# One Mamba-plus-LoRA layer on one core: the second residual is carried by an identity in the weights, the turned tiles are copied by ScalarE, and the work is ordered by new shift tables

## The chip, the cores and the metric

The kernel runs on one core of one Trainium2 chip. The metric is device time in microseconds (us) of one execution. One execution was also taken with the hardware profiler; that one gives the rows shown here. Engines are named as in the profile: PE is TensorE (PEld its weight loads), DVE is VectorE, ACT is ScalarE, POOL is GpSimd, SP is SyncE, whose queue starts every DMA of this kernel.

## What is computed

Four sequences of 512 tokens with 1024 features, all in fp32. Each sequence passes a state-space mixer and then a small feed-forward product; a layer norm with residual follows each of the two.

```python
def mixer(x):                                  # D = 2048 channels, N = 16 states, R = 64
    u, gate = split(x @ W_in.T)
    u = silu(causal_conv4(u) + conv_b)
    dt, B, C = split(u @ Wx.T, [R, R + N])     # each root-mean-square normed
    delta = softplus(dt @ Wdt.T + dt_bias)
    state_t = exp(delta * A) * state_(t-1) + (delta * u) * B   # per channel and state
    y = sum_n state * C + u * D_param
    return (y * silu(gate)) @ W_out.T

x1 = layernorm(x + mixer(x))
out = layernorm(x1 + x1 @ W.T + b + lora(x1))  # lora: rank 8, 16, 32 or 64, chosen per token
```

The second residual, the `x1 +` in the last line, is what the change touches.

## The kernel before

**The scan.** The recurrence is cut into 256 units: sequence b (4), group g of 512 channels (4), state n (16), in that order. For one unit POOL multiplies `delta_u` by a broadcast row of B (stage `drive`, L1816, 128x2048), ACT makes four decays with exp (`decay`, L1604), DVE runs four scans (`scan`, L1347, 128x512), PE turns the result in four tiles (`turn`, L1166, four 128x128 matmuls for a tile), and each turned tile is multiplied by its C column and added to `y_acc`. That last step has two ways: DVE does it in one instruction (`add`, L1372), or ACT scales the tile into a buffer (`scale`, L1624) and POOL adds it (`sum`, L1821). The first unit of a group writes `y_acc` instead (`first`, ACT).

**The work beside it.** Beside the scans run the products of the other stages: `u_mm` and `g_mm` (the input product, from weights split in a rounded part and a rest: three matmuls for each of 8 k-tiles, L1198 to L1200, called a triple here), `o_mm` (the output product, L1221), `f_mm` (the feed-forward product, triples again), the layer norms, and everything that copies and turns their results. Weights are loaded by SP to `w_raw`, rounded by ACT (`w_high`, L1645), their rest is made by POOL (`w_low`, L1840), the pair is stored once (`w_store`) and loaded ready made later (`w_load`).

**The second residual before.** For sequences 0 to 2 the feed-forward product comes out with features on the partitions. ACT copies it from its bank with the bias (`f_copy`, L1717), PE turns it (`f_turn`), and DVE adds the turned tile to `rows`, which holds x1 (`f_add`, L1426, in one line with `o_add`, the same for the first residual). The last sequence is done in the tail with tokens on the partitions: POOL adds the bias to `rows` (`fr_bias`, L1850, 128x1024 four times), and DVE adds the product's bank to `rows` (`fr_add`, L1458).

**The order.** A planner (`Plan.arrange`) fixes the order of instructions on each engine when the program is built. Each piece has a due time, an assumed length, needs, and the buffers that it takes. An engine's next piece is the one with the earliest due time among those that are ready. Due times are shifted by two tables, `STAGE_SHIFTS` (by stage and sequence) and `JOB_SHIFTS` (by job), in half microseconds. Whether an add goes to DVE or to ACT and POOL is settled in the planner too, by which of the two comes up first:

```python
put("DVE", i + 5 - ADD_FIRST, 0.645, "add", (s, tt), [*turned, summed(s - 1, tt)])
put("ACT", i + 5 - ADD_FIRST, 0.575, "scale", (s, tt), turned, take=[("scaled", (s, tt))], ahead_of="POOL")
```

At run time each engine works through its list and waits on semaphores, so an engine never goes past a piece that is not ready. Three banks of PSUM serve all products and turns beside the scan. SP too takes its list in order: `wf_load` is one piece of the planner and four DMAs (32 for a half of the ready-made feed-forward weights), and waits for the last `o_mm` of sequence 2 (first half), or for the last turns of the scan (second half).

Of the kernel before, what the change touches and what calls it, by code (L numbers as in the profile page):

```python
# [11 lines left out]
P = 128  # L12
# [5 lines left out]
GT = 4  # L18
# [89 lines left out]
class Once:  # L108
# [5 lines left out]
    def wait_ge(self, semaphore, value):  # L114
# [6 lines left out]
    "x_load": (-143, 5, 23, 103, 59, -146, -93, 156),  # L121
    "x_high": (-158, -53, -68, -77),
    "x_first": (-47,),
    "raw_load": (-53, -72, -27, -113),
    "w_high": (-41,),
    "dt_rest": (77,),
    "w_store": (61,),
    "consts": (125,),
    "lora_high": (-124,),
    "lora_rest": (78,),  # L130
    "rows_load": (215, 5, -73, -29),
    "w_low": (-31,),
# [18 lines left out]
    "delta_mm": (-4, 0, 43, -100),
    "softplus": (-160, 108, 88, 101),
    "g_mm": (41, 5, 30, 51),
    "g_copy": (-140, 113, -79, -79),
    "g_silu": (-113, -50, -82, -77),
    "g_store": (121, 13, -155, 144),
    "x_low": (0, -66, -150, -51),
    "w_load": (0, 13, 3, 19, 102),
    "o_mm": (1, 9, 68, 97),
    "o_copy": (160, -157, -110, -4),  # L160
    "o_turn": (-155, -36, -39, 113),
    "o_add": (-94, -34, -64, -118),
    "ln1_stats": (-128, -147, 87),
    "ln1_sqrt": (49, 66, 8),
    "ln1_rstd": (-40, 50, 72),
    "ln1_bias": (-160, 14, 141),
    "ln1_norm": (-142, -53, 122),
    "x1_turn": (-97, -91, 10),
    "x1_high": (72, -272, -44),
    "x1_low": (-38, -323, -43),  # L170
    "route_mm": (-60, -51, -112, -144),
    "route_lift": (-27, 90, 130, 122),
    "route_rows": (-218, -122, -45, -71),
    "route_max": (-235, -15, -97, 54),
    "route_exp": (-215, -5, 113, 63),
    "route_pick": (-213, -48, -93, -108),
    "route_mask": (29, -26, -160, 148),
    "route_turn": (-119, -109, -156, -135),
    "lora_cols": (24, 51, 34, 201),
    "lora_low": (-86, -2, -54, -65),  # L180
    "f_mm": (-3, 44, 177),
    "f_lora": (39, -152, 66),
    "f_copy": (-47, -77, -104),
    "f_turn": (9, -134, -75),
    "f_add": (17, -56, 34),
    "ln2_stats": (35, -86, -37),
    "ln2_sqrt": (72, 66, -50),
    "ln2_rstd": (-68, -132, 42),
    "ln2_bias": (-213, -233, 147),
    "ln2_norm": (-78, 157, -153),  # L190
    "y_high": (0, 0, 0, 0, 0, 0, 0, 0, 81, 7, 123, 147, 73, 28, 56, -100),
    "y_rest": (0, 0, 0, 0, 0, 0, 0, 0, 68, 83, 9, 120),
    "y_low": (0, 0, 0, 0, 0, 0, 0, 0, 0, 0, 0, 0, -97, 84, 88, 108),
    "or_mm": (115, 120, -35, 32),
    "or_table": (0, 0, 0, -95),
    "or_add": (5, 68, -150, 99),
    "or_stats": (91, 269, 66, 139),
    "or_sqrt": (-57, 119, -57, 111),
    "or_rstd": (106, 34, 36, 26),
    "or_norm": (-90, 194, 118, -14),  # L200
    "or_vnorm": (144, -40, -96, -233),
    "xr_turn": (-121, -93, 157, -95),
    "xr_high": (-43, -137, 105, -259),
    "xr_low": (-147, 191, 53, -56),
    "fr_table": (0, 0, 0, -136),
    "wf_load": (155, 59),
    "bias_load": (-76,),
    "fr_bias": (-75, 43, -76, 106),
    "fr_mm": (-208, -16, 70, 93),
    "fr_lora": (127, 69, -34, -125),  # L210
    "fr_add": (170, 150, -79, 97),
    "fr_stats": (-63, 17, 81, 129),
    "fr_sqrt": (17, -135, -158, 72),
    "fr_rstd": (-144, -132, 65, -272),
    "fr_norm": (25, -57, 77, 66),
    "fr_vnorm": (-259, 28, -48, -132),
    "rows_store": (-181, -155, 86, -65),
    "fetch": (-93, 15, 53, -141),
    "du_head": (107,),
    "g_load": (123, -18, 140, 116),  # L220
    "y_turn": (-135, 27, -103, -23),
    "y_skip": (-99, -155, 72, -11),
    "y_gate": (-118, -158, 119, 135),
    "drive_begun": (45,),
    "drive_head": (-13,),
    "decay": (-38, -16, 69, -25),
    "scan": (62, -5, -1, 79),
    "turn": (9, -157, -104, -97),
    "first": (72, -16, 0, -111),
    "drive": (95, 12, 143, 2),  # L230
    "add": (-68, -10, -43, 61),
    "scale": (-170, 30, -148, -125),
    "sum": (-113, -1, 119, -228),
    "du": (-51, -70, -59, 22),
# [3 lines left out]
    "x": (-151, -131, 34, 142, -119, -114, 42, 149, 55, -3, 38, 57, 75, -2, 86, 93, -93, 27, 26, 3, 90, 96, 90, 99, -55, -71, -158, -128, 24, -36, 38, 135),  # L238
    "split": (
# [8 lines left out]
    ),  # L248
    "u": (-121, -90, 35, 105, -39, -35, 44, 86, 36, 140, 48, -158, -137, -113, 58, -30, -33, -44, -66, -132, 4, 33, 83, 77, -110, -142, 55, -29, 113, 139, -140, 104, 44, -19, -144, -113, -61, -155, -6, -4, 140, -85, -14, -10, -34, 60, 101, -20, 67, 65, -141, 22, -15, 127, -51, 152, 64, 128, 20, -134, 48, 112, 66, 105),
# [1666 lines left out]
```

## Time and profile before

| | |
|---|---|
| runs | 2136.52, 2137.46, 2137.69 us (median 2137.46) |
| profiled execution | 2135.3 us, its span 2133.5 us |
| first scan starts, last scan ends | 137.17 us, 2027.4 us |
| DVE busy between these two | 1859.08 of 1890.25 us |
| instructions | 30661 |

The span is what the profiler saw from the first to the last instruction; 1.8 us of the execution's time lie around it. The program has three stretches: a head, in which the first sequence's products are made and no scan can run; the long middle with the scans; and a tail, the last sequence's output product, layer norms and feed-forward product. A busy share is the union of an engine's instructions, so instructions that overlap in the pipeline of their engine count once there; the mean length of one instruction is somewhat more than the step from its start to the start of the next.

### The profile page before, as it was taken

The numbers are of one execution on the slowest core, as the hardware profiler recorded it, in microseconds if no ns is written. First come the engines' busy times: TensorE is split into PE (matmuls) and PEld (weight loads), VectorE is DVE, ScalarE is ACT, GpSimd is POOL, SyncE is SP. The second block draws the span as 40 slices with busy tenths as digits, with TensorE's granted clock in tenths as the row PEclk, the third lists the DMA queues.
The fourth block names the chain that finished last, engine by engine and source line by source line (L and its number), as shares of the span: only waits on it lengthen the run. The fifth ranks groups of instructions, "written<-read, shape, count | busy, mean of one in ns | idle before, by whom it ended". The sixth has DMA issues, their size and how long they took to land.

```text
span 2133.5 us, 30661 instructions
## 1 busy us (share of the span) xinstructions
PE 2024.4 (95%) x10528; PEld 1529.3 (72%) x10528; DVE 1965.2 (92%) x2379; ACT 1477.0 (69%) x2191; POOL 1811.0 (85%) x773
## 2 busy tenths in 40 slices
PE   7999999999989799999999997999999999899998
PEld 6877778877565477788775556878875557686686
DVE  3469999999999999999999999999999999999944
ACT  4488777787576777786876557677796666857622
POOL 4369988988999999888899998988799998789941
PEclk9999999999999999999999998999999999999999
DMA  8887856654333358765563333585464337455340
GB/s 283 275 296 263 268 193 192 207 176 129 96 102 111 106 170 257 244 196 170 170 190 113 106 104 104 169 285 169 147 202 114 108 97 248 138 166 154 109 144 40
DMA packets 168763, 363.22 MB, mean 170 GB/s; under 512 B 18656, under 2 KB 45408, under 8 KB 168608
## 3 DMA queue, kind: packets, MB, share of 16 engines
q1 hardware_dynamic: 168608, 361.26, 52.9%
q8 instruction: 84, 1.38, 0.3%
q14 instruction: 71, 0.58, 0.1%
HBM read 292.35 MB, written 68.85 MB: 169 GB/s over the span
## 4 chain that ended last, share of the span: by engine, by line
PE 27%; DVE 17%; issue 5%; ACT 2%; POOL 1%; DMA 1%; SPq 1%; DVEq 0%; POOLq 0%; ACTq 0%
DVE drive L1347 10%; PE bank L1221 8%; PE state_t L1166 7%; DVE y_acc L1372 4%; PE bank L1198 2%; PE bank L1200 2%; PE bank L1199 2%; DVE channels L1379 1%; PE bank L1166 1%; POOL drive L1816 1%; DVE ln_stats L1435 1%; DVE channels L1416 1%; DMA w_split<-w_split 1%; PE bank L1264 0%; SPq L1132 0%
## 5 line engine op out<-in xcount | busy, mean ns | idle before, releaser
L1816 POOL TENSOR_TENSOR drive<-delta_u,b_bcast 128x2048 f32<-128x2048 f32 x255 | 1168.8, 4585 | 82.6 <-PE state_t L1166 76.3
L1347 DVE TENSOR_TENSOR_SCAN drive<-decay,drive 128x512 f32<-128x512 f32 x1024 | 1192.5, 1207 | 4.5 <-ACT decay L1604 3.9
L1604 ACT ACTIVATE decay<-delta,a_sb 128x512 f32<-128x512 f32 x1024 | 692.7, 688 | 352.8 <-DVE drive L1347 347.8
L1166 PEld LDWEIGHTS state_t<-identity,drive 128*128 128x128 f32 x4096 | 479.9, 142 | 251.0 <-DVE drive L1347 72.7
L1166 PE MATMUL state_t<-identity,drive 128*128 128x128 f32 x4096 | 574.9, 277 | 57.8 <-DVE drive L1347 32.7
L1198 PE MATMUL bank<-cols_high,w_split 128*128 128x512 f32 (+1 forms) x1240 | 527.2, 425 | 28.4 <-POOL w_split L1840 16.5
L1372 DVE SCALAR_TENSOR_TENSOR y_acc<-state_t,c_rows,y_acc 128x512 f32<-128x512 f32 x702 | 498.0, 736 | 20.7 <-PE state_t L1166 19.4
L1200 PE MATMUL bank<-cols_high,w_split 128*128 128x512 f32 (+1 forms) x1240 | 491.0, 396 | 0.0
L1199 PE MATMUL bank<-cols_low,w_split 128*128 128x512 f32 (+1 forms) x1240 | 488.5, 394 | 0.0
L1221 PE MATMUL bank<-channels,w_raw 128*128 128x512 f32 x896 | 421.5, 593 | 2.5 <-ACT delta L1709 2.0
L1821 POOL TENSOR_TENSOR y_acc<-y_acc,scaled 128x512 f32<-128x512 f32 x258 | 332.5, 1289 | 73.1 <-ACT scaled L1624 70.3
L1198 PEld LDWEIGHTS bank<-cols_high,w_split 128*128 128x128 f32 (+1 forms) x1240 | 235.2, 190 | 73.8 <-issue 19.5
L1200 PEld LDWEIGHTS bank<-cols_high,w_split 128*128 128x128 f32 (+1 forms) x1240 | 234.1, 189 | 54.4 <-issue 0.6
L1199 PEld LDWEIGHTS bank<-cols_low,w_split 128*128 128x128 f32 (+1 forms) x1240 | 236.3, 191 | 36.8 <-issue 0.7
L1221 PEld LDWEIGHTS bank<-channels,w_raw 128*128 128x128 f32 x896 | 153.2, 190 | 112.7 <-issue 109.9
L1624 ACT ACTIVATE scaled<-state_t,c_rows 128x512 f32<-128x512 f32 x258 | 175.8, 681 | 81.4 <-PE state_t L1166 46.9
L1840 POOL TENSOR_TENSOR w_split<-w_raw,w_split 128x512 fp32r<-128x512 f32 (+1 forms) x98 | 128.3, 1319 | 95.5 <-ACT w_split L1645 95.3
L1379 DVE SCALAR_TENSOR_TENSOR channels<-bank,conv_w_sb,channels 128x511 f32<-128x511 f32 (+2 forms) x192 | 142.7, 745 | 52.2 <-ACT channels L1653 47.6
L1604 ACT ACT_TABLE_LOAD x78 | 100.1, 1283 | 1.9 <-DVE drive L1347 0.6
L1645 ACT ACTIVATE w_split<-w_raw 128x512 fp32r<-128x512 f32 (+1 forms) x98 | 60.2, 619 | 39.2 <-PE decay L1285 10.4
L1836 POOL TENSOR_TENSOR channels<-channels,scratch 128x512 f32<-128x512 f32 x64 | 82.1, 1301 | 5.6 <-DVE channels L1416 4.4
L1829 POOL TENSOR_TENSOR delta_u<-delta,channels 128x512 f32<-128x512 f32 x60 | 75.7, 1288 | 1.8 <-ACT delta L1709 1.3
(226 smaller groups left out, 1441.4 us busy)
## 6 DMA issues: line engine op xcount, KB each, us to landing
w_split<-w_split SPq DMA_DIRECT2D x304, 512.0 KB, 4.3
b_bcast<-b_rows SPq DMA_DIRECT2D x256, 256.0 KB, 3.5
w_raw<-in_w_out SPq DMA_DIRECT2D x112, 256.0 KB, 3.0
w_raw<-in_w_in SPq DMA_DIRECT2D x64, 256.0 KB, 4.2
gates<-scratch SPq DMA_DIRECT2D x64, 256.0 KB, 3.8
scratch<-gates SPq DMA_DIRECT2D x64, 256.0 KB, 4.7
rows<-in_x_rows SPq DMA_DIRECT2D x4, 2048.0 KB, 10.7
out<-rows SPq DMA_DIRECT2D x16, 512.0 KB, 4.5
```

Of the source, the lines that this page charges most:

```text
L1166: last = engine.transpose(bank[0:tile.shape[1], i * P:(i + 1) * P], tile, identity[:, :])
L1198: engine.matmul(bank[:, :], high[:, k % WK, :], cols_high[:, k, :], start=first, stop=False)
L1199: engine.matmul(bank[:, :], high[:, k % WK, :], cols_low[:, k, :], start=False, stop=False)
L1200: engine.matmul(bank[:, :], low[:, k % WK, :], cols_high[:, k, :], start=False, stop=last).then_inc(signal[stage])
L1221: engine.matmul(bank[:, :], tile[:, k % WK, :], chan[s % 2][:, k, :], start=(k == tiles[0]), stop=(k == tiles[-1])).then_inc(signal["o_mm"])
L1347: engine.tensor_tensor_scan(state, decay[(GT * s + t) % DECAYS][:, :], state, 0.0, ALU.mult, ALU.add).then_inc(signal["scan"])
L1372: engine.scalar_tensor_tensor(y_acc[:, tt, :], bank[:, :], c, y_acc[:, tt, :], ALU.mult, ALU.add).then_inc(signal["add"])
L1379: m = engine.scalar_tensor_tensor(conv[:, back:T], bank[:, 0:T - back], conv_w[:, j, KC - 1 - back:KC - back], conv[:, back:T], ALU.mult, ...
L1604: engine.activation(decay[i % DECAYS][:, :], delta[:, g % 2, t, :], ACT.Exp, scale=a_sb[:, j, n:n + 1]).then_inc(signal["decay"])
L1624: engine.activation(scaled[:, :], bank[:, :], ACT.Copy, scale=c_rows[b % 2][:, tt, n:n + 1]).then_inc(signal["scale"])
L1816: engine.tensor_tensor(drive[key % DRIVES][:, :, :], du[:, :, :], row, ALU.mult).then_inc(signal["drive"])
L1821: engine.tensor_tensor(y_acc[:, tt, :], y_acc[:, tt, :], scaled[:, :], ALU.add).then_inc(signal["sum"])
```

## The change

The feed-forward weights get an identity added to them before they are split: for output tile h and k-tile h, POOL adds `identity` to a 128x128 part of `w_raw` (`w_eye`, eight in all, in the first use only; the stored weights carry it from then on). So the product already holds x1. `f_add` becomes a plain copy of the turned tile to `rows`, on ACT, with the same waits as before. In the tail `fr_bias` falls away: `fr_add` adds the bank to the bias tile instead of to `rows`, and takes over the waits that `fr_bias` had. Both shift tables are new in every entry, so the whole order is another one.

```diff
+def with_rows(what):
+    return F_TILE <= what[0] < ROUTE_TILE and (what[0] - F_TILE) // WK == what[1]
...
 STAGE_SHIFTS = {
-    "x_load": (-143, 5, 23, 103, 59, -146, -93, 156),
+    "x_load": (-45, -95, 18, 21, 133, 108, 80, 51),
...
-        put("ACT", due - 4, 0.13 + 0.4 * part, "w_high", w, [("raw_load", ("w", w))], take=[(pool, w)])
+        if with_rows(what):
+            put("POOL", due - 5, 0.4, "w_eye", w, [("raw_load", ("w", w))])
+        put("ACT", due - 4, 0.13 + 0.4 * part, "w_high", w, [("w_eye", w) if with_rows(what) else ("raw_load", ("w", w))], take=[(pool, w)])
...
-        put("DVE", due + 1.5, 0.585, name + "_add", key, [(name + "_turn", key), ("rows_load", key[0])] + (
+        put("DVE" if name == "o" else "ACT", due + 1.5, 0.585, name + "_add", key, [(name + "_turn", key), ("rows_load", key[0])] + (
...
-            put("POOL", at + 3, 2.4, "fr_bias", tt, [("bias_load", 0), *[("xr_turn", (tt, q)) for q in range(HT // GT)]])
...
-                put("DVE", due, 0.69, "fr_add", (tt, half), [("fr_lora", (tt, half)), ("fr_bias", tt)], give=[("bank", ("fr_mm", (tt, half)))])
+                put("DVE", due, 0.69, "fr_add", (tt, half), [("fr_lora", (tt, half)), ("bias_load", 0), *[("xr_turn", (tt, q)) for q in range(HT // GT)]], give=[("bank", ("fr_mm", (tt, half)))])
...
-                    engine.tensor_tensor(dst, bank[:, :], dst, ALU.add).then_inc(signal[stage])
+                    beside = dst if stage == "or_add" else ffn_bias[:, half * T:(half + 1) * T]
+                    engine.tensor_tensor(dst, bank[:, :], beside, ALU.add).then_inc(signal[stage])
...
+                elif stage == "f_add":
+                    s, h = key
+                    e.wait_ge(*done("f_turn", key))
+                    for h2 in range(HT):
+                        e.wait_ge(*done("x1_turn", (s, h2)))
+                    bank = banks[place["bank", ("f_turn", key)]]
+                    engine.activation(rows[:, :, h * P:(h + 1) * P], bank[:, :].rearrange("p (a q) -> p a q", a=TT), ACT.Copy).then_inc(signal["f_add"])
...
+                elif stage == "w_eye":
+                    at = (key[0][0] - F_TILE) % WK * P
+                    diagonal = raw[place["raw", key]][:, at:at + P]
+                    e.wait_ge(*done("raw_load", ("w", key)))
+                    engine.tensor_tensor(diagonal, diagonal, identity[:, :], ALU.add).then_inc(signal["w_eye"])
```

What the two orders hold that differs in number (everything else is there as often as before):

| engine, instruction | before | after |
|---|---|---|
| DVE `add` (y_acc from state_t) | 702 | 715 |
| DVE `o_add` and `f_add` (rows from a turned bank) | 64 | 40 |
| ACT `f_add` (copy to rows) | 0 | 24 |
| ACT `scale`, POOL `sum` | 258 each | 245 each |
| ACT table loads | 170 | 168 |
| POOL `fr_bias` | 4 | 0 |
| POOL `w_eye` | 0 | 8 |

Three places of the order are shown. The first is SP's queue from the program's start. `drive<-in_x_cols` loads one of the first sequence's eight k-tiles of x, `w_raw<-in_w_in` half of a weight tile; between them stand the constants, which are left out here but for the first and the last of twelve. Before:

```order
L1051 DMA drive<-in_x_cols 128x512
L1075 DMA w_raw<-in_w_in 128x512 x2
L1051 DMA drive<-in_x_cols 128x512
L1075 DMA w_raw<-in_w_in 128x512 x2
L1051 DMA drive<-in_x_cols 128x512 x5
L1045 DMA conv_w_sb<-in_conv_w 128x64
...
L1045 DMA drive<-in_lora_b 128x1024
L1051 DMA drive<-in_x_cols 128x512
```

and of the change:

```order
L1081 DMA w_raw<-in_w_in 128x512 x4
L1057 DMA drive<-in_x_cols 128x512 x7
L1051 DMA conv_w_sb<-in_conv_w 128x64
...
L1051 DMA drive<-in_lora_b 128x1024
L1057 DMA drive<-in_x_cols 128x512
```

The k-tile that is left for the end, behind the constants, was k = 7 before and is k = 4 now. Before, PE begins with two output tiles in turn, by k: ten triples stand ahead of the first that needs k = 7. Now it takes k = 0 to 3 of one tile and of a second, eight triples, and then needs k = 4.

The second place is ACT where the first scans are made ready: `delta<-bank` is softplus for two channel tiles, `decay<-delta` the exp of a scan, `dt_slot<-w_raw` and `w_split<-w_raw` round weights, `scratch<-bank` and `scratch<-scratch` copy a gate tile and take its silu. Before:

```order
L1693 ACTIVATE dt_cols<-bank,dt_ln_w_sb 128x512
L1666 ACTIVATE scratch<-bank 128x512
L1709 ACTIVATE delta<-bank,dt_bias_sb 128x512 x2
L1645 ACTIVATE w_split<-w_raw 128x512
L1604 ACT_TABLE_LOAD
L1604 ACTIVATE decay<-delta,a_sb 128x512 x2
L1645 ACTIVATE dt_slot<-w_raw 128x256
L1645 ACTIVATE w_split<-w_raw 128x512 x2
L1709 ACT_TABLE_LOAD
L1709 ACTIVATE delta<-bank,dt_bias_sb 128x512 x2
L1666 ACTIVATE scratch<-bank 128x512
L1604 ACT_TABLE_LOAD
```

and of the change:

```order
L1679 ACTIVATE scratch<-bank 128x512
L1706 ACTIVATE dt_cols<-bank,dt_ln_w_sb 128x512
L1658 ACTIVATE w_split<-w_raw 128x512
L1722 ACTIVATE delta<-bank,dt_bias_sb 128x512 x2
L1610 ACT_TABLE_LOAD
L1610 ACTIVATE decay<-delta,a_sb 128x512
L1658 ACTIVATE dt_slot<-w_raw 128x256
L1679 ACTIVATE scratch<-bank 128x512
L1658 ACTIVATE w_split<-w_raw 128x512
L1686 ACT_TABLE_LOAD
L1686 ACTIVATE scratch<-scratch 128x512 x2
L1722 ACT_TABLE_LOAD
```

The gate's silu with its table now stands ahead of the second softplus. On PE eleven gate triples stand ahead of the first `delta_mm` where eight stood (from the first `delta_mm` to the first turn of unit 1 both orders have the same 28 triples); on DVE only the first scan stands ahead of the second half of `delta_u` and `drive`, where two scans stood; on POOL 41 `w_low` stand ahead of the first `drive`, where 39 stood.

The third place is SP's queue in sequence 3, where the first half of the feed-forward weights is loaded (`w_f_early`, each row one fourth of a piece `wf_load`); `w_split<-w_split` is a `w_load`, `b_bcast` the row of B for a unit's `drive`. Before:

```order
L1078 DMA w_raw<-in_w_out 128x512
L1132 DMA w_f_early<-w_split 128x2x128 x16
L1119 DMA b_bcast<-b_rows 128x512
L1132 DMA w_f_early<-w_split 128x2x128 x4
L1097 DMA w_split<-w_split 128x1024
L1132 DMA w_f_early<-w_split 128x2x128 x8
L1097 DMA w_split<-w_split 128x1024
L1132 DMA w_f_early<-w_split 128x2x128 x4
L1119 DMA b_bcast<-b_rows 128x512
```

and of the change:

```order
L1084 DMA w_raw<-in_w_out 128x512 x2
L1138 DMA w_f_early<-w_split 128x2x128 x16
L1103 DMA w_split<-w_split 128x1024
L1138 DMA w_f_early<-w_split 128x2x128 x4
L1125 DMA b_bcast<-b_rows 128x512
L1138 DMA w_f_early<-w_split 128x2x128 x12
L1103 DMA w_split<-w_split 128x1024
L1125 DMA b_bcast<-b_rows 128x512
```

The first ready-made weight stood behind 16 DMAs, a row of B and four more, and stands behind 16 now; the second stood behind eight further ones and now follows the first by four, a row of B and twelve. In the second half of these loads (`w_f_late`, in the tail) both orders are alike: twelve DMAs, two loads of weights and the bias ahead of the last gate tile's load.

## Rows read from the trace of the kernel before

**Rows 1.** The page: engines' busy time, share of the span, instructions

```profile
PE 2024.4 (95%) x10528; PEld 1529.3 (72%) x10528; DVE 1965.2 (92%) x2379; ACT 1477.0 (69%) x2191; POOL 1811.0 (85%) x773
DVE  3469999999999999999999999999999999999944
```

**Rows 2.** Windows of head, middle, tail: busy us (instructions), clock, DMA share, GB/s

```profile
0.00:137.17 137.17, 122.20 (x583) 100.21 (x584) 57.46 (x85) 68.76 (x110) 52.84 (x45) 1.00 0.82 284
137.17:2027.42 1890.25, 1803.38 (x9482) 1349.61 (x9481) 1859.08 (x2191) 1380.23 (x2035) 1725.59 (x707) 0.99 0.52 166
2027.42:2133.50 106.08, 98.77 (x467) 79.44 (x465) 48.65 (x106) 27.99 (x47) 32.58 (x22) 0.98 0.30 93
```

**Rows 3.** Waits in the middle: total us, times, longest

```profile
ACT decay L1604 <- DVE drive L1347: 347.8, 423, 4.5
...
DVE y_acc L1372 <- PE state_t L1166: 18.0, 26, 4.1
```

**Rows 4.** Groups by line: busy us, mean ns, idle before

```profile
L1372 DVE SCALAR_TENSOR_TENSOR y_acc<-state_t,c_rows,y_acc 128x512 f32<-128x512 f32 x702 | 498.0, 736 | 20.7 <-PE state_t L1166 19.4
L1821 POOL TENSOR_TENSOR y_acc<-y_acc,scaled 128x512 f32<-128x512 f32 x258 | 332.5, 1289 | 73.1 <-ACT scaled L1624 70.3 <-PE state_t L1166 2.4
...
L1426 DVE TENSOR_TENSOR rows<-bank,rows 128x512 f32<-128x512 f32 x64 | 42.8, 675 | 0.0
...
L1775 ACT ACTIVATE cols_high<-bank 128x512 fp32r<-128x512 f32 x24 | 13.5, 594 | 0.8 <-PE bank L1166 0.7
...
L1850 POOL TENSOR_TENSOR rows<-rows,y_acc 128x1024 f32<-128x1024 f32 x4 | 9.6, 2405 | 19.3 <-PE bank L1166 16.9 <-PE state_t L1166 2.5
```

**Rows 5.** DVE's timeline near the last scan: start, length, instructions

```profile
2018.07 0.73 DVE L1372 SCALAR_TENSOR_TENSOR y_acc<-state_t,c_rows,y_acc 128x512 f32<-128x512 f32 x1
2018.71 1.22 DVE L1347 TENSOR_TENSOR_SCAN drive<-decay,drive 128x512 f32<-128x512 f32 x1
2019.84 0.68 DVE L1426 TENSOR_TENSOR rows<-bank,rows 128x512 f32<-128x512 f32 x1
2020.42 0.75 DVE L1372 SCALAR_TENSOR_TENSOR y_acc<-state_t,c_rows,y_acc 128x512 f32<-128x512 f32 x1
```

**Rows 6.** SP's timeline at the start: the last of the eight x tiles

```profile
13.25 0.43 SPq L1051 DMA_DIRECT2D drive<-in_x_cols  x1
```

**Rows 7.** PE's timeline in the head: the eleventh triple, two neighbours

```profile
20.24 0.47 PE L1198 MATMUL bank<-cols_high,w_split 128*128 128x512 f32 x1
...
38.63 0.39 PE L1198 MATMUL bank<-cols_high,w_split 128*128 128x512 f32 x1
...
39.31 0.39 PE L1198 MATMUL bank<-cols_high,w_split 128*128 128x512 f32 x1
```

**Rows 8.** PE's waits in the head: total us, times, longest

```profile
PE bank L1198 <- POOL w_split L1840: 12.9, 5, 7.4
```

**Rows 9.** PE's timeline: first `delta_mm`, first turns of unit 1

```profile
126.51 0.47 PE L1242 MATMUL bank<-dt_cols,dt_slot 128*128 128x512 f32 x1
...
151.77 1.03 PE L1166 MATMUL state_t<-identity,drive 128*128 128x128 f32 x8
```

**Rows 10.** DVE's timeline: `drive_head`, first adds of unit 1

```profile
139.41 3.67 DVE L1364 TENSOR_TENSOR drive<-delta_u,b_bcast 128x1024 f32<-128x1024 f32 x1
...
152.40 1.41 DVE L1372 SCALAR_TENSOR_TENSOR y_acc<-state_t,c_rows,y_acc 128x512 f32<-128x512 f32 x2 [2.46 <-PE state_t L1166]
```

**Rows 11.** POOL's timeline beside it: unit 1's `drive`

```profile
137.38 4.63 POOL L1816 TENSOR_TENSOR drive<-delta_u,b_bcast 128x2048 f32<-128x2048 f32 x1 [1.28 <-issue]
```

**Rows 12.** SP's timeline: the two bursts of `wf_load`

```profile
1762.29 10.37 SPq L1132 DMA_DIRECT2D w_f_early<-w_split  x16
...
2031.01 7.73 SPq L1132 DMA_DIRECT2D w_f_late<-w_split  x12
```

**Rows 13.** The chain that ended last, at the first burst

```profile
1776.83 4.87 DMA w_split<-w_split
```

**Rows 14.** DVE's timeline behind the first burst

```profile
1786.72 1.41 DVE L1372 SCALAR_TENSOR_TENSOR y_acc<-state_t,c_rows,y_acc 128x512 f32<-128x512 f32 x2 [4.12 <-PE state_t L1166]
```

More of the change, by code:

```diff
@@ L151 @@
[L151 to L165, printed above, removed]
@@ L180 @@
[L180 to L193, printed above, removed]
@@ L194 @@
[L194 to L234, printed above, removed]
+    "x_load": (-45, -95, 18, 21, 133, 108, 80, 51),
+    "x_high": (-76, -83, 54, -15),
+    "x_first": (-58,),
@@ new lines @@
+    "ssm_table": (22,),
+    "ssm_sqrt": (-53, -132, -2, -7),
+    "softplus_table": (3,),
+    "ssm_dt": (73, -53, -90, -76),
+    "ssm_norm": (-6, -107, 13, 117),
+    "ssm_turn_dt": (17, -114, 110, -111),
+    "ssm_turn_b": (16, -135, 230, 186),
+    "dt_cols": (93, 153, 25, 117),
+    "dt_low": (-47, -137, 36, -20),
+    "b_cols": (28, -83, -33, -154),
+    "b_store": (-109, 54, 106, -2),
+    "delta_mm": (19, -7, 71, -34),
+    "softplus": (5, 117, 110, 79),
+    "g_mm": (34, 13, 147, 116),
@@ L235 @@
+    "drive_begun": (-68,),
+    "drive_head": (39,),
+    "decay": (-85, 68, 150, -22),
+    "scan": (121, 5, -2, 69),
+    "turn": (6, -154, -157, 12),
+    "first": (-38, -58, -81, -74),
+    "drive": (139, 10, 84, 154),
+    "add": (-11, -9, 66, -152),
+    "scale": (-76, -59, -35, -156),
+    "sum": (-145, -95, 109, -119),
+    "du": (26, 68, 137, -41),
 }
 JOB_SHIFTS = {
-    "x": (-151, -131, 34, 142, -119, -114, 42, 149, 55, -3, 38, 57, 75, -2, 86, 93, -93, 27, 26, 3, 90, 96, 90, 99, -55, -71, -158, -128, 24, -36, 38, 135),
+    "x": (24, 95, -17, -81, 114, 93, 29, -108, -100, 51, 33, 23, 30, 66, 56, 92, -96, 2, -94, 18, 73, -7, 126, 156, 43, -41, 58, -47, 45, 81, 91, 126),
@@ L271 @@
[L271 to L275 removed]
+        (-2, 18, -97, -99), (-142, -56, -46, 86), (-61, -3, -52, -104), (-97, -2, -108, 91), (0, 12, -61, 84), (-83, 127, -106, 131),
@@ new lines @@
+    "fetch": (-150, -103, 158, -89, -84, 15, -1, 20, 31, -120, 147, 96, 126, -94, 95, -14),
+    "y": (-17, -63, -155, -150, 52, -121, 10, 123, -80, 84, 21, -124, 33, -40, -165, -144),
+    "drive_begun": (-100,),
+    "drive_head": (-132,),
+    "decay": (50, 106, 68, -18, -79, 42, 129, 45, -36, 24, 102, -6, -158, -60, -59, -137),
+    "scan": (14, 26, 36, 52, 126, 118, -11, 104, -6, 119, 148, 146, -43, -61, 57, -34),
+    "turn": (-124, 4, 71, -78, 45, 56, -118, -108, 63, -147, 155, 12, -87, -45, 117, -14),
@@ L276 @@
+    "first": (89, 150, -5, 68, 124, 71, 132, -81, -45, -108, -19, -125, -87, -122, -127, -80),
+    "drive": (-26, 136, -134, -115, 60, -15, -161, 104, 15, -98, 17, -45, -134, -126, -101, -163),
+    "add": (-49, 24, 20, 108, 85, -137, 13, 9, -210, 56, -75, -60, 85, 17, 129, 148),
+    "scale": (258, -58, -69, -128, -31, 60, -33, -97, -228, 64, 91, -12, 50, 77, 63, -9),
+    "sum": (53, 138, -115, -100, 67, -38, 23, 135, -119, 116, -141, -151, -46, -125, 40, -66),
 }
@@ L1420, in _ @@
                     e.wait_ge(*done("rows_load", s))
-                    e.wait_ge(*done(stage[0] + "_turn", key))
-                    if stage == "f_add":
-                        for h2 in range(HT):
-                            e.wait_ge(*done("x1_turn", (s, h2)))
-                    bank = banks[place["bank", (stage[0] + "_turn", key)]]
+                    e.wait_ge(*done("o_turn", key))
+                    bank = banks[place["bank", ("o_turn", key)]]
                     engine.tensor_tensor(dst, bank[:, :].rearrange("p (a q) -> p a q", a=TT), dst, ALU.add).then_inc(signal[stage])
@@ L1845, in _ @@
                     engine.tensor_tensor(y_rest[:, key, :], y, y_high_of(key).bitcast(F32), ALU.subtract).then_inc(signal["y_rest"])
-                elif stage == "fr_bias":
-                    e.wait_ge(*done("bias_load", 0))
-                    for q in range(HT // GT):
-                        e.wait_ge(*done("xr_turn", (key, q)))
-                    engine.tensor_tensor(rows[:, key, :], rows[:, key, :], ffn_bias, ALU.add).then_inc(signal["fr_bias"])
+                elif stage == "w_eye":
[3 more added lines that the diff above has]
+                    engine.tensor_tensor(diagonal, diagonal, identity[:, :], ALU.add).then_inc(signal["w_eye"])
                 elif stage == "x_low":
```

172 lines of the change are left out of this document (102 added, 70 removed), and 16 rows, old and new, of the table JOB_SHIFTS.

## Prediction

> **What bounds the kernel now.** I read the page first: PE is busy 95% of the span and DVE 92%, but DVE's slices show nine tenths or more from the fifth to the 38th and little outside them [rows 1]. An average over head, middle and tail hides the bound, so I cut the span at the first and the last scan. In the middle DVE is busy 1859.08 of 1890.25 us, 98.4%, and PE 1803.38 [rows 2]. DVE's idle time there is 31.2 us. Of that 18.0 us, in 26 waits of 4.1 at most, is for PE's turned states; ACT in the same stretch waits 347.8 us for DVE's drives [rows 3]. So DVE's own work sets the length of the middle, and a microsecond put on or taken off DVE there counts nearly whole. Head and tail are PE's: 122.20 of 137.17 and 98.77 of 106.08 us [rows 2]. DVE's timeline gives the price of one instruction as the step to the next start: an add 0.64 (2018.07 to 2018.71), a scan 1.13, an add into `rows` 0.58 (2019.84 to 2020.42) [rows 5]. The group means, 736 and 675 ns [rows 4], count the overlap twice.
>
> **Term 1: DVE's load in the middle.** The 24 `f_add` leave DVE: 24 x 0.58 = 14.0 us less. But the new order sends 13 more adds to DVE, 715 for 702. One add fewer than before stands behind the last scan, so 14 more stand ahead of it: 14 x 0.65 = 9.1 us more. Net -4.9 us. With mean lengths for steps (14 x 0.736 = 10.3 against 24 x 0.675 = 16.2) it is -5.9, and with the longest add against the shortest `rows` add -3.6; I take -4.9, since the steps are what a full engine pays.
>
> **What ACT and POOL get.** ACT copies 24 banks, which it does in 594 ns elsewhere [rows 4], +14.2 us, and loses 13 `scale` (a 128x512 activation too, about 0.6 each, -7.8) and two table loads. That is some +4 us on an engine that waits 347.8 us for DVE [rows 3]; hidden. POOL loses 13 `sum` of 1289 ns (-16.8 us) [rows 4] and gains eight `w_eye`: from 1289 ns for 512 columns and 2405 for 1024 a 128-column add costs between 0.28 (slope alone through those two) and 0.45, so 2.2 to 3.6 us. They sit beside `w_low` at a weight's first use; were one late, PE would wait for it at most its own length, 3.6 us in all. I put it at nothing. `fr_bias` takes 4 x 2405 ns off POOL in the tail, where POOL was idle 19.3 us before them [rows 4], and `fr_add` reads the bias tile, there since the head: nothing.
>
> **Term 2: the head.** The last of the eight x tiles is issued at 13.25 [rows 6], and PE's eleventh triple starts at 20.24 [rows 7], so ten triples were ready to be done without it. Now it is k = 4 that comes last, and eight triples are ahead of it: two more at 0.68 (38.63 to 39.31, [rows 7]) remain, +1.4 us. Against that PE waited 12.9 us in five waits for `w_split` in the head, 7.4 of them in one [rows 8]; the four others, 5.5 us, lie partly among the first ten triples, and a wait for x swallows about 1.8 of them. Net -0.4. Then eleven gate triples, not eight, stand ahead of the first `delta_mm` (126.51 before, [rows 9]), three more, +2.0 us; from there to unit 1's turns both orders have the same 28 triples. Net +1.6, from 0 (the waits for `w_split` hide it all) to +4 (none of it hidden, and the later second softplus, behind the gate's table, costs a stall).
>
> Two things in it are beside DVE. DVE's `drive_head` took 3.67 us [rows 10] while POOL's `drive` ran from 137.38 for 4.63 [rows 11]; it ended 1.1 us after that. In the new order POOL still has `w_low` left there, so `drive_head` may come up to 1.2 us sooner. The first adds of unit 1 wait for its turns (2.46 idle before 152.40, [rows 10]), which are PE's (151.77, [rows 9]), so a quicker `drive_head` would only lengthen that idle time; were DVE the later of the two there, the sum would be -4.1. The Trainium skill ("SBUF — State Buffer", section "Who interferes with whom") says that a VectorE instruction with both inputs in SBUF contends with GpSimd's reads, one of the two blocking while the other holds the shared port. By that rule the trace agrees at `drive_head` (3.67 us beside POOL's 4.63). It also speaks against a second gain from this change: the removed adds take one input from PSUM, so their leaving would free POOL nothing.
>
> **Term 3: the tail.** From its first product on PE is full there (98.77 of 106.08, [rows 2]). One more triple-like step of the output product stands behind the last scan, +0.7, and one add fewer, which shortens the way to it by half of 0.64: +0.4 us. The second burst of `wf_load`, 12 DMAs in 7.73 us [rows 12], stands ahead of the same loads as before: 0.
>
> **Term 4: the first burst.** Before, SP took 10.37 us for 16 DMAs from 1762.29 [rows 12], 0.65 each; the ready weight behind the burst was issued at 1776.83 and took 4.87, so landed at 1781.7 [rows 13], and DVE stood idle 4.12 us until 1786.72 [rows 14]. That is the longest of the 26. Now the first ready weight is issued behind 16 DMAs, at 10.4 from the burst's start, and lands at 15.3. Counting PE's triples at 0.68 and the turns between, it is needed at about 19.4: no stall. The second follows 18 DMAs later, 22.1, and lands at 26.9; PE needs it at about 22.9. So a stall of 4.0 us comes where one of 4.1 was: 0, between -4 (DVE has units in hand then) and +4 (the next loads are late too).
>
> **The sum.** -4.9 + 1.6 + 0.4 + 0 = -2.9 us. The profiled execution took 2135.3 us, so it would take 2132.4; the median of the runs stands 2.2 above it (2137.5), so the forecast is 2134.5 us. The runs spread over 1.2 us; I take 0.2%, 4.3 us, as what a measurement tells from no change.
>
> **The rivals.**
> - *The sum holds, 0.42.* Ratio 0.9986, 2131 to 2137 us. For it: each stretch of DVE in the middle is as long as its instructions. The change then does little because 9.1 of the 14.0 us come back as adds: DVE and ACT with POOL share them by which comes first, and DVE, freed, comes first more often.
> - *Stalls shrink too, 0.27.* All of DVE's 18.0 us waiting for PE are 26 small events of the order [rows 3]; another order can have half as many. Then -9 more, 2125.5 us; half of that gives 2130. For it: the 14.0 us are also taken off the chain bank, turn, add, of which there are only three banks. Against it: the waits are spread over the whole middle, and the longest of them, at the first burst, comes back by term 4.
> - *ACT holds the banks, 0.14 (slower).* A copy on ACT stands in one line with decays, and a decay waits for DVE on average 347.8 / 423 = 0.82 us and 4.5 at most [rows 3]. A bank whose copy stands behind such a decay is free that much later than when DVE itself took it. PE, in order, stops when the next product needs the bank, and DVE's turned states are late next. At full price that is 24 x 0.82 = 19.7 us, at half 9.9: 9.9 - 2.9 = +7, 2144.5 us. It decides the sign when new DVE idle time passes 2.9 us (0.12 per copy), and reaches a measurable loss at 7.2 (0.3 per copy). Against it: PE in the middle has 87 us of slack, and the products in the bank have due times of their own.
> - *PE takes over in places, 0.17.* DVE loses about 14 us just where feed-forward products run, in sequences 0 to 2 and the next, and PE there is the nearest engine (1803.38 against 1859.08, [rows 2]). In such a stretch the saved time turns into waiting for PE: -2.9 becomes 0 to +3, 2137.5 to 2140.5.
>
> **How the numbers follow.** Likeliest: 2134.5. Its own range is 2131 to 2137, so it lies mostly within 0.2% of 2137.5, that is above 2133.2. Faster by over 0.2%: a third of the first case (0.14), nearly all of the second (0.25): 0.39. Slower: three quarters of the third case (0.11) and a third of the fourth (0.06): 0.17. Within: 0.44. The range that leaves out a tenth on each side goes from 2127 (below it the better part of the stalls would have to go) to 2142 (above it ACT would have to hold banks at over a third of full price).
>
> **What the profile of the changed kernel would show.** Term 1: DVE's group of adds with 715, the group into `rows` with 40, DVE busy in the middle near 1854. Term 2: the wait for x behind the eighth triple, unit 1's first adds near 154.0 for 152.40. Term 3: a tail of 106.5. Term 4: no idle time behind the first ready weight, some 4 us behind the second. Stalls: the wait of `add` for `state_t` under or over 18.0. ACT holding banks: PE waiting for `rows` from ACT, which no view of before has. Wrong it would be above all if DVE's idle time in the middle, 31.2 us now, moved by more than 5 us either way, or if the adds' 14 were not what the profile counts.

## The result, and the profile after

The changed kernel takes 2145.64 us (median of 6 runs, 2143.24 to 2148.86), the kernel before 2136.77 in the same comparison: ratio 1.0045, interval 1.0035 to 1.0055. It is slower by 9 to 10 us, where 2134.5 was forecast and 2142.0 was the top of the range. The profiled execution took 2143.24 us. Three single executions in the runs below took 4138, 6592 and 7254 us; the ratios leave them out, and no median moves by more than 0.8 us with them.

The page and three windows of the changed kernel (head, middle from the first to the last scan, tail), against [rows 1, 2]:

```profile
PE 2023.3 (94%) x10528; PEld 1529.6 (71%) x10528; DVE 1960.3 (92%) x2368; ACT 1478.4 (69%) x2200; POOL 1785.8 (83%) x764
...
0.00:135.22 135.22, 122.67 (x589) 102.05 (x590) 56.84 (x82) 66.07 (x107) 49.42 (x44) 1.00 0.83 284
135.22:2035.77 1900.55, 1802.35 (x9475) 1347.68 (x9473) 1856.24 (x2181) 1384.49 (x2046) 1713.86 (x703) 0.99 0.52 166
2035.77:2141.40 105.63, 98.29 (x467) 79.85 (x466) 47.27 (x106) 27.88 (x47) 22.53 (x18) 0.99 0.30 93
```

The middle holds all of the loss: 1900.55 us for 1890.25. DVE's work in it fell by 2.8 us, its idle time rose by 13.1, from 31.2 to 44.3. Head (-1.95) and tail (-0.45) are shorter. The groups of the changed kernel's trace, as [rows 4]:

```profile
L1353 DVE TENSOR_TENSOR_SCAN drive<-decay,drive 128x512 f32<-128x512 f32 x1024 | 1193.1, 1204 | 16.7 <-POOL drive L1829 7.9 <-ACT decay L1610 7.7
L1378 DVE SCALAR_TENSOR_TENSOR y_acc<-state_t,c_rows,y_acc 128x512 f32<-128x512 f32 x715 | 504.5, 733 | 17.7 <-PE state_t L1172 16.9
...
L1429 DVE TENSOR_TENSOR rows<-bank,rows 128x512 f32<-128x512 f32 x40 | 26.6, 670 | 0.0
...
L1648 ACT ACTIVATE rows<-bank 128x512 f32<-128x512 f32 x24 | 14.1, 589 | 2.1 <-PE bank L1172 2.0
...
L1863 POOL TENSOR_TENSOR w_raw<-w_raw,identity 128x128 f32<-128x128 f32 x8 | 4.2, 520 | 0.5 <-DMA w_raw<-in_w_ffn 0.5
```

Adds wait no more than before. What grew is the wait of scans, 16.7 us of idle time before them: 7.9 us for POOL's drives, 0.2 before, and 7.7 for ACT's decays, 3.9 before. Two places of it, in the timelines of DVE, SP and POOL of the changed kernel: unit 1's first scan, and the scan of unit 226 behind SP's burst.

```profile
148.15 4.57 DVE L1353 TENSOR_TENSOR_SCAN drive<-decay,drive 128x512 f32<-128x512 f32 x4 [2.36 <-POOL drive L1829]
...
1811.43 0.60 SPq L1125 DMA_DIRECT2D b_bcast<-b_rows  x1
1812.07 7.71 SPq L1138 DMA_DIRECT2D w_f_early<-w_split  x12
...
1815.81 4.57 POOL L1829 TENSOR_TENSOR drive<-delta_u,b_bcast 128x2048 f32<-128x2048 f32 x1 [3.38 <-DMA b_bcast<-b_rows]
1820.41 1.22 DVE L1353 TENSOR_TENSOR_SCAN drive<-decay,drive 128x512 f32<-128x512 f32 x1 [2.23 <-POOL drive L1829]
```

### The profile page after: what moved, and what is told of

Same layout as the page of the kernel before. It is cut to its first block and busy times, and to the rows that moved or that the text cites. A ratio compares the mean times of both kernels' runs of the same rounds, so it can differ in the third digit from the quotient of the medians.

```text
span 2141.4 us, 30601 instructions
## 1 busy us (share of the span) xinstructions
PE 2023.3 (94%) x10528; PEld 1529.6 (71%) x10528; DVE 1960.3 (92%) x2368; ACT 1478.4 (69%) x2200; POOL 1785.8 (83%) x764
## 5 line engine op out<-in xcount | busy, mean ns | idle before, releaser
L1353 DVE TENSOR_TENSOR_SCAN drive<-decay,drive 128x512 f32<-128x512 f32 x1024 | 1193.1, 1204 | 16.7 <-POOL drive L1829 7.9
L1378 DVE SCALAR_TENSOR_TENSOR y_acc<-state_t,c_rows,y_acc 128x512 f32<-128x512 f32 x715 | 504.5, 733 | 17.7 <-PE state_t L1172 16.9
L1834 POOL TENSOR_TENSOR y_acc<-y_acc,scaled 128x512 f32<-128x512 f32 x245 | 315.7, 1289 | 69.6 <-ACT scaled L1630 67.2
L1630 ACT ACTIVATE scaled<-state_t,c_rows 128x512 f32<-128x512 f32 x245 | 166.9, 681 | 72.4 <-PE state_t L1172 42.1
L1666 ACT ACTIVATE channels<-bank,conv_b_sb,conv_w_sb 128x512 f32<-128x512 f32 x64 | 49.5, 773 | 43.1 <-PE bank L1206 42.9
```

Of the source, the lines that this page charges most:

```text
L1353: engine.tensor_tensor_scan(state, decay[(GT * s + t) % DECAYS][:, :], state, 0.0, ALU.mult, ALU.add).then_inc(signal["scan"])
L1378: engine.scalar_tensor_tensor(y_acc[:, tt, :], bank[:, :], c, y_acc[:, tt, :], ALU.mult, ALU.add).then_inc(signal["add"])
L1630: engine.activation(scaled[:, :], bank[:, :], ACT.Copy, scale=c_rows[b % 2][:, tt, n:n + 1]).then_inc(signal["scale"])
L1834: engine.tensor_tensor(y_acc[:, tt, :], y_acc[:, tt, :], scaled[:, :], ALU.add).then_inc(signal["sum"])
```

## The experiments

Two kinds of edit are used. Shift tables or code are changed and the planner makes a new order; or the order is frozen: after `plan.arrange()` a few entries `(time, stage, key)` of `plan.work` are moved from one engine's row to another's, or along it, by the planner's clock, and all else keeps its place. Ratios are to the kernel before as it ran beside each version, and the interval in brackets is 95%; the medians of before lie between 2135.4 and 2136.8 us there. Where work is left out, so is a part of the result: such a version is there for its time alone.

### The residual without the new order, and the new tables without the residual

**graft** takes the order of before and moves the residual alone:

```diff
     plan.arrange()
+    moved = [x for x in work["DVE"] if x[1] == "f_add"]
+    work["DVE"] = [x for x in work["DVE"] if x[1] != "f_add"]
+    work["ACT"] = sorted(work["ACT"] + moved, key=lambda x: x[0])
...
+            eyes.append((min(now, max(now - 5, begun["raw_load", ("w", key)] + 3)), "w_eye", key))
...
+    work["POOL"] = sorted([x for x in work["POOL"] if x[1] != "fr_bias"] + eyes, key=lambda x: x[0])
```

> The order of before, kept as it is on every engine, with only the second residual changed: the 24 f_add stand in ACT's row instead of DVE's at the place that the planner's clock gave them, eight w_eye stand on POOL ahead of their w_high, fr_bias is gone. 702 adds stay 702. Theory A (the new order is what costs; the identity itself saves DVE's time): DVE's load falls by 24 x 0.58 = 14 us and nothing fills it; some of it turns into waits, so 2123 to 2130 us against 2136.8 before. Theory B (the copies on ACT cost more than they free, since decays and banks wait behind them): no gain, 2137 to 2145 us, with new waits of PE or DVE for ACT.

2141.51 us, 1.0030 (1.0019 to 1.0040): slower than before, against theory A. DVE lost 11.0 us of work in the middle, but its idle time rose from 31.2 to 47.2 us, nearly twelve of them in units 64 to 95. The timelines of ACT, POOL, PE and DVE of graft there:

```profile
798.96 0.63 ACT L1672 ACTIVATE w_split<-w_raw 128x512 fp32r<-128x512 f32 x1 [3.21 <-POOL w_raw L1877]
...
793.93 4.59 POOL L1843 TENSOR_TENSOR drive<-delta_u,b_bcast 128x2048 f32<-128x2048 f32 x1
798.48 0.46 POOL L1877 TENSOR_TENSOR w_raw<-w_raw,identity 128x128 f32<-128x128 f32 x1
...
797.13 0.40 PE L1227 MATMUL bank<-lora_rest,lora_b_sb 128*128 128x512 f32 x1
801.41 1.09 PE L1186 MATMUL bank<-identity,scratch 128*128 128x128 f32 x4 [3.88 <-ACT scratch L1744]
802.15 0.78 PE L1218 MATMUL bank<-cols_high,w_split 128*128 128x512 f32 x1
802.72 0.63 PE L1219 MATMUL bank<-cols_low,w_split 128*128 128x512 f32 x1
...
806.80 0.75 DVE L1392 SCALAR_TENSOR_TENSOR y_acc<-state_t,c_rows,y_acc 128x512 f32<-128x512 f32 x1 [5.31 <-PE state_t L1186]
```

and graft's windows around the pause:

```profile
796.00:800.00 4.00, 1.53 (x10) 1.00 (x8) 2.92 (x4) 1.04 (x2) 4.00 (x3) 1.00 0.52 200
800.00:807.00 7.00, 5.59 (x20) 4.84 (x21) 1.42 (x2) 4.66 (x9) 4.94 (x3) 0.53 0.19 59
```

`w_eye` stands on POOL behind a drive of 4.6 us; `w_high` waits 3.21 us for it on ACT, with a copy, decays and `f_copy` queued behind; PE stands still for 3.88 us. After this pause PE runs at its lower level, 1.2 GHz (granted clock 1.00, then 0.53), and a matmul takes 0.63 us for 0.39 until 807. DVE's next add, at 806.80, has waited 5.31 us.

**graft_no_eye** is graft with `w_eye` left out of `work["POOL"]` and this wait:

```diff
-e.wait_ge(*(done("w_eye", key) if with_rows(key[0]) else done("raw_load", ("w", key))))
+e.wait_ge(*done("raw_load", ("w", key)))
```

> As graft, but w_eye is left out, so x1 is left out of the second residual; w_high waits for its load alone, as before. In graft DVE lost 10.3 us of load in the middle and got 17 us of idle time, 11 of them between units 64 and 96, where eight w_eye stand between a load and its w_high and wait there for POOL's drives of 4.6 us. Theory C (w_eye is what made graft slow): that idle time goes, 2126 to 2132 us. Theory B (the copies on ACT are): little changes, 2138 to 2143 us.

2135.91 us, 0.9997 (0.9988 to 1.0006). For a profile the same kernel was run once more, as graft_no_eye_b:

> The kernel of graft_no_eye once more, for its profile: that of the first run was of an execution of twice the usual length. Either DVE's idle time in the middle is up by about the 10 us that it was freed of, spread over all units (then PE or ACT is next in line everywhere), or it is up in a few places where a copy on ACT is late. The time as before, 2133 to 2138 us.

2135.35 us, 1.0001 (0.9992 to 1.0009). Without `w_eye` graft is 6 us faster, and just as fast as before, though DVE has 11.1 us less to do in the middle (1847.98 us in the second profile) and ACT's copies are there.

**graft_eye_dve** has `w_eye` in DVE's row:

```diff
-    work["POOL"] = sorted([x for x in work["POOL"] if x[1] != "fr_bias"] + eyes, key=lambda x: x[0])
+    work["POOL"] = [x for x in work["POOL"] if x[1] != "fr_bias"]
+    work["DVE"] = sorted(work["DVE"] + eyes, key=lambda x: x[0])
```

> As graft, but the eight w_eye stand in DVE's row, one us of the planner's clock ahead of their w_high. DVE pays 8 x about 0.2 us and is never longer than 1.2 us in one instruction. Theory C: 2128 to 2133 us, faster than before. Theory B: 2138 to 2143 us.

2144.13 us, 1.0033 (1.0021 to 1.0046): missed by 11 us. The eight took 9.7 us of DVE where 1.6 was expected. Their group, and two of them beside POOL:

```profile
L1442 DVE TENSOR_TENSOR w_raw<-w_raw,identity 128x128 f32<-128x128 f32 x8 | 9.7, 1208 | 0.0
...
705.12 4.54 POOL L1849 TENSOR_TENSOR drive<-delta_u,b_bcast 128x2048 f32<-128x2048 f32 x1
707.72 2.08 DVE L1442 TENSOR_TENSOR w_raw<-w_raw,identity 128x128 f32<-128x128 f32 x1
...
750.54 0.27 DVE L1442 TENSOR_TENSOR w_raw<-w_raw,identity 128x128 f32<-128x128 f32 x1
750.74 4.62 POOL L1849 TENSOR_TENSOR drive<-delta_u,b_bcast 128x2048 f32<-128x2048 f32 x1 [0.79 <-PE state_t L1187]
```

It takes 0.27 us when it starts ahead of POOL's drive, and 2.08 when it starts within one: it ends at 709.80, and the drive at 709.66. Six of the eight start within a drive, and each ends 0.14 to 0.16 us behind it. That is the contention of the Trainium skill, "SBUF — State Buffer", section "Who interferes with whom": a VectorE instruction with both inputs in SBUF waits while GpSimd holds the shared port. The trace agrees.

**old_tables** is all of the new code with the tables of before, **new_tables_only** the reverse:

> All of the new code, with the shift tables of before (w_eye gets 0), so the planner makes a third order: 715 adds on DVE, as in the changed kernel, and 24 copies on ACT. DVE's load is that of the changed kernel to about 1 us. Theory A: the time goes by the DVE idle time that this order happens to leave; with the 31 us of before it would be near 2133 us, with the 44 us of the changed kernel near 2145. Theory B: the copies are there, so it is at or above 2143 us whatever the tables.

> All of the code of before, the residual still added by DVE, with the new shift tables (fr_bias gets 0): 720 adds and 24 f_add on DVE. Theory A: DVE has the load of the changed kernel plus 14.0 us for f_add and 3.2 for five more adds, and an order no better: 2155 to 2165 us. Theory B: no copies on ACT, so waits go away again: 2137 to 2148 us.

2206.41 us, 1.0329 (1.0314 to 1.0343), and 2342.22 us, 1.096 (1.0945 to 1.0975). DVE is idle 76 and 138 us between the first and the last scan. Both lie far outside what either theory said and tell nothing about the copies: with these tables and the other version's pieces the planner's order has far more idle time than either of the two kernels. From here on only frozen orders were compared.

### What the copies and `w_eye` cost in the new order

**copy_on_dve** moves the 24 copies from ACT's row to DVE's (first line), **copy_small** leaves them on ACT and cuts them (the next two), **after_no_eye** takes `w_eye` out (the last):

```diff
+    plan.work["DVE"] = sorted(plan.work["DVE"] + moved, key=lambda x: x[0])
...
-engine.activation(rows[:, :, h * P:(h + 1) * P], bank[:, :].rearrange("p (a q) -> p a q", a=TT), ACT.Copy)
+engine.activation(rows[:, :, h * P:h * P + 1], bank[:, :].rearrange("p (a q) -> p a q", a=TT)[:, :, 0:1], ACT.Copy)
...
+    plan.work["POOL"] = [x for x in plan.work["POOL"] if x[1] != "w_eye"]
```

> The order of the changed kernel, kept as it is, with the 24 copies of the turned tiles moved from ACT's row to DVE's at the same place of the planner's clock. Theory A: DVE pays them, 24 x 0.58 = 14 us, less what falls into its 44 us of idle time: 2152 to 2160 us. Theory B: ACT is freed of them, so decays come earlier and banks are given back sooner: 2137 to 2146 us.

> The order of the changed kernel, kept as it is, with each of the 24 copies on ACT cut from 512 columns to 4 (so rows keeps old values in the rest, and the residual and the product are left out of it). ACT gets 24 x about 0.4 = 10 us back and the banks come free as much earlier. If the copies' length on ACT costs anything: 2136 to 2143 us. If ACT's slack covers it: 2144 to 2147 us.

> The order of the changed kernel, kept as it is, with the eight w_eye taken out of POOL's row (x1 is left out of the second residual); w_high waits for its load alone. In graft the same step brought about 6 us. Theory C (POOL's w_eye between a load and its w_high is costly in any order): 3 to 7 us less than the changed kernel, 2138 to 2142 us. Rival (the new tables load these weights early enough to hide it): 2144 to 2147 us.

2157.50 us, 1.0102 (1.0088 to 1.0116): 12 us more than the changed kernel, 0.5 per copy. 2146.23 us, 1.0040 (1.0027 to 1.0053), and 2145.64 us, 1.0047 (1.0035 to 1.0058): neither differs from the changed kernel. So in the new order the length of the copies on ACT is covered (copy_small keeps their place and their waits), and so is `w_eye`; the theories B and C fall for it.

### Taking work off DVE, and putting it on

**before_small_add** cuts `f_add` on DVE to 4 columns in the kernel before. **before_adds** turns 13 pairs of `scale` and `sum` of before into one `add`; **reroute** does the opposite with five adds of the changed kernel. The edits of the first two:

```diff
+                    if stage == "f_add":
+                        dst, turned_bank = dst[:, :, 0:1], turned_bank[:, :, 0:1]
...
+    for key in [(72, 2), (76, 1), (78, 0), (89, 3), (93, 2), (130, 0), (134, 2), (142, 3), (150, 2), (161, 0), (169, 2), (174, 1), (181, 1)]:
+        at = next(x[0] for x in work["ACT"] if x[1:] == ("scale", key))
+        work["ACT"] = [x for x in work["ACT"] if x[1:] != ("scale", key)]
+        work["POOL"] = [x for x in work["POOL"] if x[1:] != ("sum", key)]
+        work["DVE"].append((at, "add", key))
```

> The kernel before, its order kept, with each of DVE's 24 f_add cut from 512 columns to 4 (the second residual and its product reach one column in 128). ACT gets no copies and POOL no w_eye, DVE has about 24 x 0.45 = 11 us less to do. If DVE's load sets the middle, as the prediction had it: 2125 to 2129 us. If what DVE is freed of turns into waits for PE, ACT or POOL, as graft_no_eye hints with 10 us less on DVE and no gain: 2132 to 2136 us, and the copies on ACT are then not to blame.

> The kernel before, its order kept, but 13 of its 258 pairs of scale (ACT) and sum (POOL) are one add on DVE instead, as many as the changed kernel has more: five in units 64 to 95, four in 128 to 159, four in 160 to 191, where the changed kernel has them. Theory E (the adds are the loss; DVE pays what is put on it in full though what is taken off it brings nothing): 13 x 0.65 = 8.5 us more, 2142 to 2146 us. Rival F (the adds fall into idle time or shorten the way of a state, and the loss is the new order's late pieces): 2135 to 2139 us.

> The changed kernel, its order kept, but five of its 715 adds are a scale on ACT and a sum on POOL instead, at units 118, 119, 170, 182 and 187, where ACT and POOL were free by the planner's clock. Theory E: 5 x 0.65 = 3.3 us less, 2141 to 2143.5 us. Rival F: 2144 to 2147 us.

before_small_add: 2134.87 us, 0.9996 (0.9987 to 1.0005), no measurable gain for 9 us less on DVE; the interval leaves room for 2.8 us. before_adds: 2142.70 us, 1.0033 (1.0021 to 1.0045), by the ratio a loss of 7.0 us (4.5 to 9.6), 0.54 for each add that goes from ACT and POOL to DVE. reroute: 2146.51 us, 1.0049 (1.0037 to 1.0061), no gain again. What is put on DVE costs about its step of 0.64 us, what is taken off it brings little or nothing. Why shows in the windows of units 80 to 95, where the first eight `f_add` stand, in the kernel before and then in before_small_add (busy us of PE, PEld, DVE, ACT, POOL):

```profile
726.00:855.80 129.80, 117.84 (x659) 93.66 (x659) 128.70 (x175) 99.73 (x154) 128.69 (x63) 0.98 0.61 200
```

```profile
726.70:856.30 129.60, 117.57 (x659) 93.95 (x659) 125.33 (x174) 99.62 (x154) 128.50 (x63) 0.98 0.61 202
```

DVE and POOL are both busy for 128.7 of 129.8 us. With 3.4 us taken off DVE the stretch is 0.2 us shorter: it is POOL's, whose drives, sums, `w_low` and other pieces stand there almost without a gap. In units 160 to 191, where the second eight stand, PE is second in line. Windows of before and of before_small_add:

```profile
1320.30:1575.90 255.60, 249.94 (x1433) 208.97 (x1434) 251.89 (x301) 188.56 (x276) 219.08 (x93) 0.99 0.58 189
```

```profile
1322.40:1576.60 254.20, 248.65 (x1433) 208.39 (x1434) 248.65 (x302) 188.08 (x276) 219.08 (x93) 1.00 0.57 190
```

3.2 us less on DVE gave 1.4. The third eight stand in units 224 to 255. Windows of before and of before_small_add:

```profile
1796.80:2026.20 229.40, 218.97 (x1135) 159.53 (x1134) 226.40 (x282) 166.42 (x254) 208.72 (x86) 0.99 0.47 150
```

```profile
1796.60:2024.80 228.20, 217.90 (x1136) 159.09 (x1135) 223.47 (x282) 166.23 (x254) 209.12 (x86) 0.99 0.47 151
```

Here no second engine is as full: PE stands 7.4 us below DVE. Still only 1.2 us came of 2.9. DVE's wait for PE's turned states grew from 2.3 us in 3 waits to 3.5 in 9, so the turns were late one by one though PE was not full on average. A full second engine is therefore shown as the reason in the first stretch, fits in the second, and does not explain the third.

### SP's burst

**spread** changes SP's row of the changed kernel, **before_spread** that of the kernel before, **spread_reroute** joins spread and reroute:

```diff
+    spread = [x for x in work["SP"] if x[1] == "wf_load" and x[2][0] == 0]
+    later = [(spread[0][0] + 8 * i, *x[1:]) for i, x in enumerate(spread)]
+    work["SP"] = sorted([x for x in work["SP"] if x not in spread] + later, key=lambda x: x[0])
```

> The order of the changed kernel; only SP's row is changed: the eight pieces of wf_load for the first half follow each other every 8 us of the planner's clock instead of in one burst of 32 DMAs. In the changed kernel DVE is idle 5.2 us behind the burst in three scans whose drive waited for a late row of B. Theory D (SP's burst costs what stands behind it in the queue): 4 to 6 us less, 2139 to 2142 us. Rival: the loads contend with others wherever they are, or the lost time comes back as another wait: 2143 to 2147 us.

> The kernel before, with only SP's row changed in the way of spread: the eight pieces of wf_load for the first half follow each other every 8 us of the planner's clock. Before, DVE was idle 4.1 us behind the burst. Theory D (SP's burst costs what stands behind it): 3 to 5 us less, 2131 to 2133 us. Rival (in this order the wait comes back elsewhere): 2135 to 2138 us.

> The changed kernel with both edits, of spread and of reroute. Theory E with D: they add up, 2136 to 2138 us. If only the burst counts: as spread, 2139 to 2141 us.

spread: 2139.68 us, 1.0015 (1.0006 to 1.0024), 6 us off the changed kernel. before_spread: 2130.28 us, 0.9975 (0.9966 to 0.9983), 5.1 us less than the kernel before and the fastest version found. spread_reroute: 2144.06 us, 1.0036 (1.0024 to 1.0048), 4.4 us above spread by the medians. The two don't add up. Whether the second costs anything is open: the intervals of spread and spread_reroute meet at 1.0024, and reroute alone changed nothing. In the changed kernel 5.2 of the 7.9 us of waits for POOL's drives stood behind the burst. The waits of DVE in the middle in spread:

```profile
DVE y_acc L1382 <- PE state_t L1176: 18.3, 26, 2.2
DVE drive L1357 <- ACT decay L1614: 8.0, 11, 2.1
DVE drive L1357 <- POOL drive L1833: 2.8, 2, 2.4
```

and in before_spread, where the 4.1 us of [rows 14] are gone from the 18.0 of [rows 3]:

```profile
DVE y_acc L1376 <- PE state_t L1170: 12.3, 21, 2.5
```

The planner counts a `wf_load`, four DMAs, as 1.0 us of SP; 16 DMAs took 10.37 us [rows 12], so it is 2.6 for four.

## Why the prediction was wrong

**The step that failed** is in the first paragraph: "a microsecond put on or taken off DVE there counts nearly whole". The half about putting on holds (before_adds 0.54 us for each add, copy_on_dve 0.5 for each copy). The half about taking off does not (before_small_add, graft_no_eye: 9 and 11 us off DVE, nothing measurable gained). The windows of the whole middle gave DVE 98.4% and POOL 91%, an average again: where the first eight `f_add` stand, POOL is as full as DVE, and where the second eight stand, PE is 2 us short of it. The prediction named the sign by which this would show, DVE's idle time moving by more than 5 us: it moved by 13.1.

**Term 1.** The load was sized about right: -2.8 us busy for -4.9 forecast. Without `f_add` DVE has 11.1 us less for the 14.0 of the sum, probably since an instruction that must now wait no longer overlaps its neighbour. But the two parts don't cancel: by the experiments the work removed counts about 0 and the adds 7.0, so the term is +7 and not -5. Those 12 us are about the size of the error, 11.1 us (2145.6 against 2134.5). Both prices were measured in the order of before. That they hold in the new one is argued, not shown, and reroute won none of it back.

**What ACT and POOL get.** Right for this order: ACT's work in the middle grew by 4.3 us for the 4 forecast, and copy_small and after_no_eye change nothing. The eight `w_eye` took 4.2 us, over the 2.2 to 3.6. But "at most its own length, 3.6 us in all" was wrong as a bound for `w_eye`: in graft it cost 6 us, since what it waits for is a drive of 4.6 us, and the wait passes to ACT, PE and PE's clock.

**Term 2, the head,** was right in size at the second unit: unit 2's first scan starts 1.5 us later than before (155.2 for 153.7). That is luck in part, for the way there is another. PE waits 0.35 us for k = 4 where +1.4 was counted, and the first `delta_mm` starts 0.6 us later (127.07 for 126.51) where 1.6 was forecast. The first scan starts 1.95 us earlier, since it now stands ahead of the second half of `delta_u`. Before, that half stood ahead of it (135.65 to 137.25), and only the second half of `drive` stood behind two scans, other than the section on the change has it. `drive_head` took 2.20 us for 3.67, as forecast. Then DVE waits 2.36 us for POOL's drive of unit 1, behind three `w_low`, and 0.97 for PE's turns, instead of 2.46 for the turns alone. **Term 3:** -0.45 for +0.4; in the tail no `fr_add` waits for the bias. **Term 4:** the burst's two weights were seen, but not the row of B between them. PE does wait 2.57 us for the second weight, of which at most 0.65 reaches DVE; the late rows of B cost DVE 5.2 us for the 4.1 of before, so +1.

**The rivals.** The one about PE taking over came nearest, with the right mechanism for part of the middle, but POOL, the engine that is just as full in units 80 to 95, was in none of them. ACT holding the banks did not happen: no PE instruction waits for one of the copies. By these prices adds +7.0, `f_add` and `w_eye` 0, burst +1 and tail -0.5 give 7.5 of the 8.9 us measured. That fits, but the trace of the changed kernel does not show the loss where this ledger would put it. By the starts of the scans the changed kernel is 6.7 us ahead of the kernel before at unit 96 (849.1 for 855.8) and 10.6 behind at unit 192 (1586.5 for 1575.9). In these 96 units, 17.3 us longer than before, DVE has 6.3 us more to do and is idle 11.0 us more. Units 128 to 159 are the plainest case, because no `f_add` stands there in either order. Their windows before and in the changed kernel:

```profile
1094.40:1320.30 225.90, 211.99 (x981) 131.93 (x979) 224.09 (x275) 148.51 (x224) 209.23 (x82) 0.97 0.38 113
```

```profile
1096.40:1328.00 231.60, 225.96 (x1077) 146.90 (x1075) 226.89 (x278) 156.75 (x234) 207.33 (x82) 1.00 0.42 128
```

Four more adds stand there, 2.2 us by the price of before_adds, and the stretch is 5.7 us longer. The new order also moved 14 us of PE's work into it. So a part of the loss belongs to the new order as a whole; how large it is no run separates, and the cause stays open to that extent.

## What to carry to other kernels

In a kernel whose engines are balanced, "DVE is 98% busy" prices only work that is added to DVE. Before crediting a saving, take the windows of just the stretches where the removed instructions stand, and look at the second-fullest engine there. Take the distance to it as a ceiling and not as the price: here it was 0.0, 2.0 and 7.4 us, and the gains in one profiled execution each were 0.2, 1.4 and 1.2. And a router that fills a freed engine with other work can turn a saving that was worth nothing into a cost that counts: keep the routing and the order fixed when an edit frees an engine, and change them in a step of its own.

## What the runs showed of the hardware

A 128x128 add of two SBUF operands on DVE took 0.27 us when it started ahead of POOL's drive and up to 2.08 when it started within one; all six that did ended 0.14 to 0.16 us behind the drive. A pause of 3.9 us of PE was followed by a stretch at half the clock (granted 0.53 over 7 us), in which matmuls of 0.39 us took 0.63, and the engine behind waited 5.3 us. SP took 10.37 us to start 16 DMAs of `w_f_early` in a row, 0.65 each; spreading that burst gained 5.1 us before and 6 in the changed kernel.
